# Other counts in the table of filling matmuls, decoder of two layers with routed experts

## What is computed

```
x = layernorm(x + nystrom_attention(x))         # 16 heads, 64 landmarks, 6 pseudo-inverse steps
x = layernorm(x + dilated_attention(x, ctx))    # 3 branches, dilation 1, 2, 4
x = layernorm(x + ternary_ffn(x))               # 256 -> 1024 -> 256, weights in {-1, 0, 1}
x = layernorm(x + fast_weight_memory(x))        # 4 heads, chunked scan with decay
x = layernorm(x + gated_cross_attention(x, ctx))# rotary, audio and text keys, then norm + relu(linear)
x = layernorm(x + routed_experts(x))            # top 2 of 8 experts, 1024 hidden
```

## Time and profile before

| | |
|---|---|
| median of three runs | 1688.19 us |
| the profiled execution, its own time | 1695.37 us |
| its span, first to last instruction | 1693.3 us |
| granted TensorE clock, mean | 0.934 of full |
| TensorE matmul busy | 1430.2 us, 84% |
| VectorE busy | 1095.3 us, 65% |
| ScalarE busy | 652.5 us, 39% |
| GpSimd busy | 296.7 us, 18% |
| fillings, line 599: loads of weights recorded | 262 |

### The profile page before, as it was taken

How to read it: one execution, slowest core, us unless ns; L and a number is a source line. 1 busy time by engine, 2 the same in 40 slices (tenths; PEclk the granted TensorE clock), 3 DMA queues, 4 the chain that set the end, 5 groups by cost and what they waited for, 6 DMA issues and landing times. The chain is left out here.

```text
span 1693.3 us, 45878 instructions
## 1 busy us (share of the span) xinstructions
PE 1430.2 (84%) x19556; PEld 1162.7 (69%) x19588; DVE 1095.3 (65%) x2483; ACT 652.5 (39%) x1349; POOL 296.7 (18%) x335
## 2 busy tenths in 40 slices
PE   5997996779898777898996879988773899999993
PEld 4995773559776555796774549767542799999882
DVE  5776676556856846576677556756845565655874
ACT  3313444332144343213443323144341564555771
POOL 0002130120202202002130020202202012122232
PEclk8799998989999898899998989999996899999997
DMA  7331120010000001000000010000001878788844
GB/s 274 125 134 81 39 81 13 15 38 4 3 3 1 26 2 40 14 4 2 3 13 13 14 40 4 2 3 1 1 2 55 300 244 291 242 276 269 268 126 112
DMA packets 50385, 134.51 MB, mean 79 GB/s; under 512 B 5121, under 2 KB 28929, under 8 KB 49153
## 3 DMA queue, kind: packets, MB, share of 16 engines
q1 hardware_dynamic: 39993, 116.75, 19.4%
q0 software_dynamic: 7152, 9.57, 2.8%
q10 hardware_dynamic: 3040, 5.26, 0.8%
HBM read 117.80 MB, written 32.13 MB: 89 GB/s over the span
## 5 line engine op out<-in xcount | busy, mean ns | idle before, releaser
L739 PE MATMUL bank<-arena 64*64 64x80 f32 (+2 forms) x6400 | 222.7, 229 | 3.9 <-DVE arena L878 2.4
L739 PEld LDWEIGHTS bank<-arena 64*64 64x64 f32 x6400 | 216.5, 140 | 13.1 <-issue 7.2
L1058 POOL TENSOR_TENSOR rstd<-ve,neghalf 128x2 f32<-128x2 f32 x48 | 37.4, 779 | 717.5 <-DVE ve L1036 716.7
L2218 PE MATMUL m_bank<-e_xT,e_w 128*128 128x256 bf16 x1440 | 161.2, 274 | 2.1 <-DVE e_xT L2319 2.1
L2218 PEld LDWEIGHTS m_bank<-e_xT,e_w 128*128 128x128 bf16 x1440 | 141.5, 98 | 19.8 <-DVE e_xT L2319 2.9
L2314 DVE TENSOR_TENSOR e_w<-e_raw,e_w 128x1024 bf16<-128x1024 f32 x90 | 108.8, 1223 | 39.7 <-ACT e_w L2258 39.5
L2334 DVE TENSOR_TENSOR e_h<-m_bank,e_silu 128x256 f32<-128x256 f32 x120 | 50.7, 422 | 89.8 <-ACT e_silu L2279 89.8
L599 PE MATMUL bank<-c_bf 128*128 128x512 bf16 x230 | 72.8, 466 | 32.3 <-ACT arena L982 10.0
L2279 ACT ACTIVATE e_silu<-m_bank 128x256 f32<-128x256 f32 (+1 forms) x192 | 65.7, 344 | 86.8 <-PE m_bank L2218 79.6
L2258 ACT CAST e_w<-e_raw 128x1024 bf16<-128x1024 f32 x90 | 92.3, 1042 | 17.9 <-DMA e_raw<-E 17.9
L1002 ACT COPY arena<-bank 128x320 f32<-128x320 f32 (+1 forms) x96 | 37.5, 391 | 159.6 <-PE bank L739 159.3
(11 more groups left out here) (317 smaller groups left out, 2972.1 us busy)
## 6 DMA issues: line engine op xcount, KB each, us to landing
e_raw<-E SPq DMA_DIRECT2D x144, 512.0 KB, 8.8
slots<-C_empty SPq DMA_DIRECT2D x13, 1360.0 KB
e_x<-slots SPq DMA_DIRECT2D x15, 272.0 KB, 8.0
w_rest<-W_rest SPq DMA_DIRECT2D x1, 3592.0 KB, 16.7
xz<-xT SPq DMA_DIRECT2D x8, 256.0 KB, 2.7
x<-x SPq DMA_DIRECT2D x8, 256.0 KB, 2.9
ctx<-ctxT SPq DMA_DIRECT2D x8, 256.0 KB, 2.7
tokens<-y SPq DMA_DIRECT2D x8, 256.0 KB, 2.1
```

The costliest lines, as they stand in the source:

```text
L739: last = pe.matmul(b[r, p * width:(p + 1) * width], lhs[r, 4 * g + p, :], rhs[r, 4 * g + p, :], start=True, stop=True)
L2218: last = pe.matmul(bank[b][:, col:col + wide], w, x, start=j == 0, stop=j == len(terms) - 1)
```

## The change

Seven of the thirteen strings in `FILLED_WAITS` are replaced; nothing else is.

```
 FILLED_WAITS = {
-    "d_coef0": "07070707",
+    "d_coef0": "09090909",
     "n_max1_0": "00909090",
     "n_aT_0": "00909090",
-    "n_xT": "09090909",
-    "g_m00_0": "09090909",
+    "n_xT": "011011011011",
+    "g_m00_0": "026026026026",
     "g_negT": "90909090",
-    "n_negT": "90000000",
+    "n_negT": "150000000",
     "n_max3_0": "00303030",
-    "d_s0_0": "01010101",
-    "g_s01_0": "10101010",
+    "d_s0_0": "02020202",
+    "g_s01_0": "10102010",
     "g_o0": "30202020",
     "g_o1": "03030303",
-    "m_xT": "06050509",
+    "m_xT": "1061051051013",
 }
```

## The result

| | before | changed |
|---|---|---|
| median of four timed runs | 1689.01 us | 1699.18 us |
| lowest and highest of them | 1686.45, 1691.05 | 1695.02, 1700.06 |
| ratio of changed to before | | 1.0052 [1.0034, 1.007] |
| the profiled execution, its own time | 1695.37 us | 1695.02 us |
| its span; mean granted clock | 1693.3; 0.934 | 1693.1; 0.926 |

The change costs 0.52%, 8.8 us; the forecast was 7.9. The two profiled executions are equally long all the same. The one of before (1695.37 us) lies above its timed runs, the one of after is the lowest of its four. So no difference of the two spans says what the change costs. It has to be read place by place, and over more than one trace of each kind.

What follows compares the result with a forecast made beforehand. Each site was taken as decided by whether TensorE waits anyway, whether the clock falls without fillings, and a fall's cost. 3.9 + 2.2 + 0.5 + 0.5 + 0.8 = +7.9 us on 1688.19 gave 1696.1 us, range 1688.5 to 1703.

Steps and rivals of the forecast that it cites:

- The count: Whole table: strings are read one character per batch, giving 212 fillings where the old table gave 262, not 401.
- the last rival: Table read with two-digit figures, 401 fillings; 26 at g_m00_0 end the low stretch: near -8 us, 1680 us; chance 0.01.
- Term 1: n_xT, odd batches: idle gaps of about 3 us bring three new clock falls at 1.31 us each, +3.9 us.
- The first rival: n_xT: the low stretch lasts longer, each of three falls costs 2.79 us; +12.4 us in all, 1700.6 us; chance 0.18.
- Term 2: g_m00_0 and n_xT, batches 2 and 4: ten fillings where TensorE does not wait delay the work, +2.2 us.
- a chain without slack: g_m00_0, batches 2 and 4: eight fillings delay VectorE's next lot by their full length, 1.7 us.
- Term 3: n_negT: batch 0 loses eight fillings for nothing, batch 1 gets five in busy work; +0.5 us, bounds -0.6 and +2.1.
- dense work may bring the clock back sooner: n_negT, batch 1: sooner recovery of the clock could offset the five fillings' 2.1 us by at most 2.7 us.
- Term 4: m_xT, batches 1 and 3: transposes start earlier, -3.1 us, but line 614 runs at the lower clock; +0.5 us net.
- Term 5: m_xT, batch 7: without fillings, logits and transposes run at the lower clock, +0.8 us, bounds 0 and 0.8.
- At nothing: Sites priced at zero: d_coef0, d_s0_0, g_s01_0, g_m00_0 in odd batches, and six at m_xT in batch 2.
- The fall stays: m_xT, batch 2: six fillings leave 1.85 us idle, so the clock still falls; if they prevented it, -1.8 us.

Runs made afterwards that it cites:

- The table as meant: Kernel before with the new figures as lists, two-digit counts kept, other strings as in the change, 401 fillings: 0.9945, -9.2 us.
- the 26 at the maxima: Kernel before with only g_m00_0 changed, to 26 fillings in the odd batches, 330 in all: 0.9972, -4.7 us.
- the fuller m_xT: Kernel before with only m_xT changed, to 10 6 10 5 10 5 10 13, 306 fillings in all: 0.9971, -4.9 us.
- n_xT alone: Kernel before with only n_xT changed, 0 1 1 0 1 1 0 1 for 0 9 0 9 0 9 0 9, 231 fillings: 1.0019, +3.2 us.
- nine in all batches: Kernel before with only g_m00_0 changed, to nine fillings in every batch, 298 in all: 1.0024, +4.0 us.
- all but n_xT: Changed kernel with n_xT put back to 0 9 0 9 0 9 0 9, 243 fillings, against the kernel before: 1.0015, +2.5 us.

## Why the prediction was right, and where its steps were not

**The count.** Right: 212 fillings, one character to a batch. The table as meant gives -9.2 us, near the -8 of the last rival, but by luck in part: that rival had it all from the 26 at the maxima, which give -4.7 alone, and the fuller m_xT, which it did not price, gives the other -4.9.

**Term 1.** The falls came as forecast: with no filling or one the clock fell in 16 of 16 batches (the changed kernel twice, n_xT alone, no fillings), with four in 4 of 4, with nine in 7 of 32 over eight kernels, with eleven in 0 of 4. The price was read from one fall and was too low in the mean. Against the undisturbed stretch (55.4 us in batch 1, 54.32 in the others) the twelve falls of the changed kernel's two traces and n_xT alone cost 1.6 us in the mean, after the 0.21 for d_s0_0 is taken off. They come in two sizes: six with a low stretch of 3.4 us at 0.7 to 1.4, six with 6.8 us at 2.1 to 2.6. Before's chance falls are worth 0.34 a batch in the mean over its 32, so the term is 4 x (1.62 - 0.34) = +5.1, not +3.9. The mean rests on the fastest of four and the slowest of nine executions of the changed kernel and one middle one of n_xT alone; the first trace by itself would have given 3.6 less 0.8 for d_s0_0, so 2.8, which is too low again.

The rule of the Trainium skill ("TensorE: Matmul & The Clock Gate", Terms) gives, as an estimate, 1.7 us for the short and 3.4 for the long stretch. The measured 1.05 and 2.24 (means of six each) are about two thirds of that; that part of the slower work lies beside VectorE's is my reading, and no run shows it. At 835.4 before, where VectorE waited for TensorE, the fall of 3.4 us cost 1.7, as much as the rule says.

**The first rival, a longer low stretch,** was half true. It came in 6 of 12 places and cost 2.2 us rather than 2.79. That 2.79 was misread: batch 5 does its work in another order than batch 3 and takes 1.1 us more with no fall too (49.22 against 48.11 us over those five norms, after), so the dearest single fall had cost 1.7. Its ground was the wrong one: the work behind the gap is the same in the short and the long case, so transposes and 32-row matmuls alone do not decide it. What does, I can't say.

**Term 2.** +2.2 was forecast. The ruler shows +1.1 for the six and two at g_m00_0 and 0.2 each for the two single ones at n_xT in batches 2 and 4 (24.40 against 24.22 us), +1.5 together. (In the four traces with two at batch 4 the stretch is 65.6 to 66.1 us, in the others 64.5 to 65.6.) What failed is "a chain without slack": VectorE has some of it, as the 0.85 us of wait for 1.3 us of fillings shows, and nine in all batches too. Odd batches are unchanged, as forecast.

**Term 3.** +1.5 us by the means of the stretch above (23.9 against 22.4), forecast 0.5. The step that was off is "dense work may bring the clock back sooner": it did so in one of four traces.

**Term 4.** The size depends on where one looks. From the last norm of batch 0 to VectorE's line 810 batch 1 is as long as before (31.3 against 31.4 us); to its line 821, behind the slow projections of line 614, it is 34.7 to 35.4 us in four traces against 33.3 to 33.8 in the seven with six fillings, +1.4 where 0.5 was forecast for batches 1 and 3. The transposes start 1.4 us or more earlier, and a slow line 614 takes back more than that.

**Term 5.** +1.3 us, forecast 0.8. From y of batch 7 to the end of the logits it takes 4.5 us in all five traces with none there, and 3.2 in four of the seven with nine. The bound was too tight, since its two prices came from places that were at the lower clock only in part: it had 1.57 us for the logits and 0.94 for the transposes, and here they take 1.88 and 1.08. Against the 1.06 and 0.66 of before that is 1.24 of the 1.3 us; the wait between them is 0.67 us in both. Timeline of TensorE after:
```profile
1285.79 1.08 PE L606 MATMUL bank<-s_ident,y 128*128 128x128 f32 x4 [4.58 <-issue]
1287.54 1.88 PE L1802 MATMUL bank<-w_rest,res 128*128 128x8 f32 x8 [0.67 <-ACT res L1819]
```

**At nothing.** Two steps failed here, with opposite signs. "The fall stays" for the six at m_xT in batch 2: the clock held in two of the four traces with six (the first of the changed kernel and all but n_xT) and fell in the other two, where it fell in all eight with none there. The stretch is 1.2 us shorter in the mean (20.2 against 21.4, the kernel with no fillings at all left out), but both sides scatter (19.48, 20.51, 19.06, 21.93 with six; 20.02 to 22.02 with none), and by line 821 in batch 3, its share of term 4 included, the gain is 0.3. I had named the -1.8 and put it aside, by counting what idleness was left (1.80 us) as if it were the old 3.15. And the filling at d_s0_0, which I laid into a wait for the exponentials, has no cover: 4 x 0.21 = +0.85 us.

A third place was not thought of: the fall in batch 5 in front of the feed-forward part. The clock fell there in 11 of 11 other kernels with fillings and held in both traces of the changed one, -1.7 us, though neither half of the change shows it alone. Why, stays open.

**The sum.** With batches 1 to 3 read at line 821: 5.1 + 1.5 + 1.5 + 1.4 - 0.3 + 1.3 + 0.85 - 1.7 = +9.65 us by places; read at line 810, where batch 1 is -0.15 and batches 2 and 3 are -1.3, it is +7.1. Measured were +8.8 and +6.5 in two series. It is no closer account than that: the stretches through the pseudo-inverses, which have no term, differ by several us between traces (252 to 257 us in three with the changed m_xT, 245 to 251 in four with the old one, all on chips with short waits at line 836), and those in front of n_xT go partly the other way (97 to 99 against 100 to 102). The forecast of 7.9 stood between the two measurements, partly by luck: the misses in terms 1, 3, 4 and 5 and at d_s0_0 (some +4.5 at line 821) were met by those in term 2, in batch 2 and in batch 5 (-2.7).

**Why the two traces are of one length.** Before's profiled execution had two low stretches that after's has not, at 125.4 to 128.8 and at 835.4; the stretches with them are 1.6 and 1.7 us longer than after's. The first is taken for chance (three of the other twelve traces have it), the second came in every other kernel with fillings and in neither trace of the changed one. The start of before's trace is 1.1 us longer, the stretches in front of n_xT 1.1, and those of m_xT in even batches 2.9, most of it the held clock in batch 2. On the other side stand n_xT +3.6, the gated stretches +1.1, the pseudo-inverses +0.7 and the end +2.8. The sum is -0.2. So what two executions differ by at places that the change does not touch or does not decide (1.1 + 1.6 + 1.1, and up to 2.9 at m_xT) is nearly as much as the whole change.

## What to carry to other kernels

A filling table is priced site by site: whether the engine waits there anyway, how long it is idle without fillings, and what stands behind the wait. A site has to be filled until little idleness is left (0.7 to 0.9 us held in the batches read here, 2.2 at n_xT in none), for four fillings of nine bought nothing there; where nothing waits, a filling is a delay of up to its length. Where chance moves single executions nearly as much as the change does, read the same place in many traces, or take a price for one that came up by luck.

## What the runs showed of the hardware beyond what I expected

- **How often a given idleness ended in a fall.** At n_xT, behind dense work: 0.74 us, no fall in 4; 1.17 us, 7 falls in 32; 2.24 us, 4 in 4; 3.1 us, 16 in 16. At m_xT in even batches: 0.93 us, none in 8; 1.80 us, 2 in 4; 3.1 us, 44 in 44. In front of line 623 in batch 5: 2.41 us, 11 in 13, the two that held being the changed kernel's.
- **The low stretch comes in two lengths,** 3.4 and 6.8 us, for the same instructions behind the same gap, sometimes within one execution (batch 7 against 3 after). One trace shows 1 long of 4, another of the same kernel 4 of 4.
- **Fillings at the lower clock may not be lost.** Without the nine at g_m00_0 and at g_negT, the low stretch lasted 20 to 27 us in place of 10, with TensorE busy for only 10.92 of 23.7 us in batch 1, and the kernel with no filling anywhere lost 2.1%. That it is the nine of g_negT, which ran at the lower clock, that brought the full one back is not shown, since no run took them away alone.
